# Moving two more picked rows per tile, one of group 9 and one of group 11, from VectorE's weighted sum to TensorE's

## The reference

```python
x = L0_attn_u
x = _layernorm(x + _L0_attn_ref(x, ...), axis=-1)   # projection, conv of 4 taps, SSD scan, gate, out projection
x = _layernorm(x + _L0_ffn_ref(x, ...), axis=-1)
...
h = act(einsum('btd,cd->btc', hidden_states, W_up) + b_up)      # 512 -> 2048
h = einsum('btc,pc->btp', h, W_down) + b_down                   # 2048 -> 256
# 8 heads: the best 8 of 64 keys twice, their 64 sums, the best 8 of these: 64 rows of 4096 a token
z = einsum('btd,bthkd->bthk', h, down_embed[indices])
z = act(z * softmax(sc, axis=-1))
out = einsum('bthk,bthkd->btd', z, up_embed[indices])
```

## Time and profile before

| what | us |
|---|---|
| median of 3 runs (lowest, highest) | 3157.48 (3154.82, 3172.02) |
| the profiled execution, time | 3151.04 |
| its span, first to last instruction | 3149.2 |
| PE busy in it | 2790.8 (89%) |
| DVE busy | 2777.5 (88%) |
| ACT busy | 2049.7 (65%) |
| POOL busy | 2062.7 (65%) |
| mean granted clock of PE | 0.953 of full speed |

### The profile page before, as it was taken

The page is one execution under the profiler, slowest core; times in us unless marked ns, Lnnn a source line. Parts: engine busy times, 40 slices in busy tenths (PEclk is TensorE's granted clock), DMA queues, the critical chain, the costliest instruction groups (busy, mean ns, idle before and its releaser), DMA issues.

```text
span 3149.2 us, 44785 instructions
## 1 busy us (share of the span) xinstructions
PE 2790.8 (89%) x11776; PEld 1737.3 (55%) x11776; DVE 2777.5 (88%) x10160; ACT 2049.7 (65%) x6513; POOL 2062.7 (65%) x2056
## 2 busy tenths in 40 slices
PE   7989899998898999999899989899898999898863
PEld 4565456655555655555566545556555565555541
DVE  3489899998899999999899989999999999899986
ACT  3466766666776666676666676666676666677642
POOL 0066666676676667666667666666766666766676
PEclk9999999999999999999999999999999999999986
DMA  8088888888888888888888888888888888888888
GB/s 284 23 263 275 270 279 273 277 290 282 272 285 265 270 292 287 276 282 277 265 277 297 273 276 271 273 278 290 284 277 268 276 272 288 283 278 281 277 303 272
DMA packets 189855, 856.76 MB, mean 272 GB/s; under 512 B 36192, under 2 KB 39392, under 8 KB 189088
## 3 DMA queue, kind: packets, MB, share of 16 engines
q0 software_dynamic: 163840, 805.44, 77.0%
q1 hardware_dynamic: 19104, 34.87, 3.2%
q10 hardware_dynamic: 6656, 13.60, 1.2%
HBM read 845.38 MB, written 8.39 MB: 271 GB/s over the span
## 4 chain that ended last, share of the span: by engine, by line
PE 38%; DVE 32%; DMA 9%; POOL 9%; issue 7%; ACT 5%; POOLq 0%; SPq 0%; DVEq 0%; ACTq 0%
DVE bank L1143 14%; POOL ring L276 9%; DMA ring<-embed,idx 9%; PE bank L500 8%; DVE ring L1129 8%; PE bank L359 7%; DVE xc L974 6%; PE bank L339 5%; PE bank L441 4%; PE bank L488 4%; PE bank L368 3%; ACT xc L679 1%; PE bank L376 1%; PE bank L307 1%; ACT xskip L691 1%
## 5 line engine op out<-in xcount | busy, mean ns | idle before, releaser
L276 POOL DMA_INDIRECT ring<-embed,idx x2048 | 2061.4, 1007 | 1074.8 <-issue 532.3
L1143 DVE SCALAR_TENSOR_TENSOR bank<-ring,coef,bank 128x512 f32<-128x512 f32 x1312 | 992.4, 756 | 7.4 <-issue 0.2
L1129 DVE SCALAR_TENSOR_TENSOR ring<-ring,hcur 128x256 f32<-128x256 f32 x2048 | 823.8, 423 | 138.5 <-DMA ring<-embed,idx 136.1
L645 ACT ACTIVATE coef<-prob,zp 128x1 f32<-128x1 f32 x2048 | 456.0, 286 | 630.8 <-DVE ring L1129 625.4
L500 PE MATMUL bank<-ring,diag_c 128*128 128x512 f32 x1344 | 672.8, 631 | 115.9 <-ACT diag_c L654 101.3
L463 PE MATMUL bank<-zs,w_up 128*128 128x128 f32 x4096 | 502.2, 287 | 69.2 <-ACT zs L767 65.8
L463 PEld LDWEIGHTS bank<-zs,w_up 128*128 128x128 f32 x4096 | 496.2, 203 | 110.2 <-ACT zs L767 91.8
L500 PEld LDWEIGHTS bank<-ring,diag_c 128*128 128x128 f32 x1344 | 247.2, 199 | 379.2 <-issue 223.7
L974 DVE SCALAR_TENSOR_TENSOR xc<-raw,taps,xc 128x128 f32<-128x128 f32 x960 | 266.2, 351 | 102.6 <-ACT xc L679 102.5
L339 PE MATMUL bank<-w_in,ut 128*128 128x512 f32 (+1 forms) x768 | 285.8, 524 | 4.0 <-ACT seg L667 3.9
L654 ACT ACTIVATE diag_c<-cst,coef 128x128 f32<-128x128 f32 x672 | 234.8, 394 | 48.4 <-PE bank L500 38.0
(11 more groups left out here) (144 smaller groups left out, 3422.2 us busy)
## 6 DMA issues: line engine op xcount, KB each, us to landing
ring<-embed,idx POOLq DMA_INDIRECT x2048, 4.6
ring<-uT SPq DMA_DIRECT2D x4, 2048.0 KB, 14.2
ut<-uT SPq DMA_DIRECT2D x32, 256.0 KB, 6.5
zs<-u SPq DMA_DIRECT2D x32, 256.0 KB, 5.6
out<-acc SPq DMA_DIRECT2D x32, 256.0 KB, 4.6
w_up<-W_upT ACTq DMA_DIRECT2D x1, 4096.0 KB, 13.0
w_in<-W_in ACTq DMA_DIRECT2D x1, 2560.0 KB, 17.4
w_in<-W_in ACTq DMA_DIRECT2D x1, 2048.0 KB, 22.0
```

The lines of the kernel that those rows point to most:

```text
L276: pool.indirect_dma_start(out=ring[:, k % RING, :], out_offset=None, in_=embed, in_offset=bass.IndirectOffsetOnAxis(ap=idx[:, half, k:k + ...
L645: m = act.activation(coef[:, k:k + 1], prob_v[:, k:k + 1], ACT.Silu, scale=zp[:, k:k + 1])
L1129: m = dve.scalar_tensor_tensor(out=ring[:, k % RING, 0:DP], in0=ring[:, k % RING, 0:DP], scalar=1.0, in1=hcur[:, :], op0=ALU.mult, op1=ALU ...
L1143: dve.scalar_tensor_tensor(out=total if n == len(DVE_ROWS) - 1 else running[:, :], in0=ring[:, k % RING, DP:ROW], scalar=coef[:, k:k + 1], ...
```

## The change

One row of group 9 (k = 26) and one of group 11 (k = 32) change their letter from D to P. Everything else follows from the strings: PE has 23 rows a tile instead of 21 and DVE 41 instead of 43; `weighted` now does one row at `old(9)` and one at `old(11)`; ACT makes two more diagonals a tile; DVE weighs two rows of group 9 instead of three (between the dots of group 11), and three rows of group 11 instead of four (between the dots of group 13). PE signals 12 groups a tile instead of 10, and POOL waits for PE instead of DVE before it gathers row 39 (into the place of row 26) and row 45 (into that of row 32).

```diff
-GROUPS = ("DD", "PPPD", "DD", "DDD", "PPD", "DDD", "DD", "DDD", "PDDD", "DDD", "DDD", "DDDD", "PDD", "PPPD", "PP", "PDD", "PPPP", "D", "DDD", "PPPD", "D", "PDD")
+GROUPS = ("DD", "PPPD", "DD", "DDD", "PPD", "DDD", "DD", "DDD", "PDDD", "PDD", "DDD", "PDDD", "PDD", "PPPD", "PP", "PDD", "PPPP", "D", "DDD", "PPPD", "D", "PDD")
```

## The result

The kernel after takes 3208.66 us (median of 6 runs, 3206.79 to 3214.7) against 3156.91 for the kernel before, measured beside it (median of 6, 3148.27 to 3172.02): a ratio of 1.0163 with a 95% interval of 1.0138 to 1.0188. It is slower, and the forecast of 3218 is 9 us too high. The profiled execution took 3212.14 with a span of 3210.3, so it is 61.1 longer than the profiled execution of before; the sum had said 61. The medians differ by only 51.8, because the profiled execution of before was 5.9 under the median now measured for its kernel and that of after 3.5 above its own.

A forecast was written before the change was run, and what follows sets the result against it. Bound: a chain of waits through DVE, PE and gathers. Terms 17 x 3.03 + 5 x 1.87 + 7 x 0.52 = 64.5, less 1.3 for the last tile, taken as 61; 3157.5 + 61 = 3218, range 3172 to 3242.

The forecast's parts named there:

- First stretch: From the convolution to h, where DVE ends last: h 0.82 us late in tile A, 0.34 earlier in tiles with slack.
- DVE's lead: Before h, group 9's lost weighing (0.66 us) brings h only 0.34 earlier, because row 38's landing limits it.
- tiles with slack: Tiles where PE's wait for h covers group 9's row, so PE reaches group 13 only 0.52 us later.
- Group 11's row: On PE between the transpose of h and `key_scores`, without cover: 0.86 us.
- DVE's weighing of row 32: Between group 13's dots, behind h: losing it gains 0, as DVE then waits for `key_scores` or row 52; bound 0.66.
- The swap: At L991, which moves 0.64 us ahead, the blocked gather becomes row 59's instead of row 60's: 1.99 more a tile.
- Rival 1: PE is late as worked out, but the blocked gather stays row 60's: 35 us, so 3192; chance 0.15.
- tile A: Tile of the kernel before, low clock on `up_proj`, PE's wait for h 0.57 us; forecast 3.03 more, in 17 tiles.
- Rival 2: Group 9's row, before `down_proj`, is hidden in all tiles and only 0.52 is paid: 15 us, so 3173; chance 0.11.
- Rival 3: Both rows hide on PE and DVE's lead passes through L991 to row 60's gather: -19 us, so 3138; chance 0.05.
- Rival 4: PE's low clock goes away because PE idles less: about 3142, or 3150 if a few stretches remain; chance 0.03.
- Rival 5: The low clock lies on `up_proj` in each tile, all becoming like tile A: 88 us, so 3245; chance 0.09.

The follow-up runs named there:

- e1b: Kernel before with only row 26 (group 9) moved from DVE to PE: 3164.43 us, ratio 1.0021.
- e2b: Kernel before with only row 32 (group 11) moved from DVE to PE: 3199.26 us, ratio 1.0137.
- e9: Kernel before with L988's masked product in PSUM and `skip_term` put behind groups 16 and 17 in ACT's order: 3110.34 us, ratio 0.985.

## Why the prediction was right, by its own steps

- **First stretch.** Right in what it says of h; DVE's lead was mis-sized. DVE's idle time before L1047 is 1.00 in the tile shown, and it was ready 27.79 - 1.00 = 26.79 behind the convolution, so only 0.18 earlier and not 0.34: the wait for a landing is at row 36's dot (0.28), not at row 38's. In a tile where h is late this lead is worth nothing, so the term did no harm there. In the six tiles with slack the transpose comes about 0.5 earlier in three, where the sum has 0.34, and 0.1 to 1.1 later in the other three. That DVE waits here and PE's row makes it wait is shown by e1b and e2b: with row 26 the wait is there, without it not.
- **Group 11's row, 0.86 on the path.** Right: 84.07 - 82.08 = 1.99 in the tile shown, and 1.99 to 2.00 with row 32 alone in 27 of the 29 tiles (in the other two the low clock lies there). ACT's copy of the transpose covers nothing.
- **DVE's weighing of row 32, worth 0 behind a landing.** Right. Row 52's dot waits 0.23 for its DMA, and with row 32 left on DVE (e1b) it does not.
- **The swap.** Right, in 29 tiles of 29, with L991 0.23 to 0.49 ahead of the gather (0.34 on average; forecast 0.2 to 0.4). Row 52's gather is 1.19 later on average (the sum has 1.20), L991 only 0.75. Rival 1 has fallen. The step rested on a margin of 0.21, and e1b shows how thin that is: there tiles fall on both sides. The prediction's words on rival 1, that L991 led row 59's gather by over 0.2 in all seven tiles of before, are not right: in one it led by 0.08. In four others it led by 0.01 to 0.02, and the gather was not blocked.
- **Size.** 2.22 a tile was forecast for row 60's dot, from 64.5 / 29, and it came to 2.06. Two terms make it up. The first, how much later L991 comes, has 0.71 in the sum and measured 0.75. Two things that were not in the sum nearly cancel in it: more tiles have the low clock on `up_proj` than before (23 against 18), which is the dear pattern; and the tiles in which it fell behind h went from 5 to 1, which gives back about 1.7 in each. The second term, the swap, was mis-sized. Its 1.99 was read from one tile of each kind. Over the 29 tiles of before it is 8.10 from L991 to row 60's dot where row 59's gather is the blocked one (7 tiles) and 6.39 where row 60's is (22 tiles); after the change it is 8.12. So the swap costs 1.7 in each of these 22 tiles. By the dot of row 63 only 1.84 of the 2.06 are left: the gather of row 61 waited 0.47 for PE in tile A and now comes, behind the longer blocked one, without a wait. So another 0.2 was cover for another wait. That the whole came out at 61.1 is luck: from the transpose of h in the third pass to that in the next to last one, 28 passes, it is 52.4 more (forecast about 62), before them 3.4 and behind them 5.3 (forecast about 1 for the two together). What the ends of the program lost was not followed up.
- **From the difference to the median.** The 9 us by which 3218 is too high come from here. The difference between two profiled executions was added to a median, and such a difference has the scatter of two single executions in it, here 5.9 + 3.5.
- **Rival 2** (group 9's row hidden) has fallen with 24 waits of L1047. **Rival 3** needed the row behind the transpose to hide, and it doesn't. **Rival 4:** the mean granted clock stays at 0.953; low stretches changed place, but their share of the time is the same. **Rival 5** was partly true: 23 tiles have the low clock on `up_proj`, more than the 18 of before, but not all 29.
- **Where my expectations failed.** I took the swap to come with either row alone, since each moves L991 against the gathers a little. In e2b, where it came in every tile, DVE gained on PE between h and L991 (row 59's gather is 0.32 behind L991 on average, 0.09 ahead before). Row 26's delay of h moves both. Over the 29 tiles of e1b the transpose comes 0.29 later than before on average, only 8 us in all, because in the tiles where h isn't late it comes earlier than before; row 60's dot comes 0.39 later. The profiled executions of e1b and of before differ by 19.5 us, a tile of e1b taking 94.11, but the medians of many runs by only 7.9; which of these a tile's account should meet stays open. The sum was right for the change as a whole, and could not be split by row.

## What to carry to other kernels

A row moved between two busy engines is priced by the wait that ends last at each place that it touches, and by the order in which those places then meet: here about half of the cost, by the subtraction above, was a gather pushed behind a VectorE instruction that blocks it. When several waits lie within some tenths of each other, work out which event overtakes which, and expect the removal of one to show the next; only the two edits of e9 together gave 1.5%.

## What the runs showed of the hardware

- In the kernels before and after, a gather that starts while L991 runs (a `tensor_tensor` over 128x2048 with two inputs in SBUF, 2.29 us) and at least 0.06 behind its start takes 1.9 to 3.0 us on POOL instead of 0.95, and in each of the three rows shown of after and e1b it ends 0.81 to 0.82 after L991 does. One that starts 0.16 before it takes 0.95. The order is decided within some hundredths of a microsecond: in before and e1b the gathers that started up to 0.04 behind L991 still took 0.95, and the next ones, at 0.06 to 0.08, took 3.0. With one of the inputs in PSUM the gather takes 0.94 and L991 still 2.29 us. VectorE is busy 2749.1 us with this edit on the kernel after and 2750.0 without, so the block costs POOL alone, and the cure costs VectorE nothing. By the Trainium skill (SBUF — State Buffer, "Who interferes with whom") this instruction should leave descriptor generation alone, which the page marks as inferred. Here the gather as a whole is held up. But it also reads its indices (`idx`) from SBUF, and no run tells whether that read or the making of the descriptors is what waits.
- On one chip the same program took 3652 us instead of 3157, at a granted clock of 0.89 to 0.91 instead of 0.953, with pauses inside matmul groups that the profile puts down to issue. What causes them stays open.
